# Loading the later fixed expert weights pair by pair instead of in groups of four pairs

## What is computed

```
x = x + attn_a(layernorm(x));  x = x + ffn(layernorm(x))
x = x + attn_b(layernorm(x));  x = x + ffn(layernorm(x))      # the same ffn weights

# ffn, with n = 2048 tokens, E = 64 experts, 256 -> 64 -> 256 features
g = silu(einsum('nd,edf->nef', flat, wg))
u = einsum('nd,edf->nef', flat, wu)
routed = einsum('ne,nef,efd->nd', comb, g * u, wd)
shared = einsum('nsh,shd->nd', silu(flat @ swg) * (flat @ swu), swd)
```

## Time and profile before

| | |
|---|---|
| time, median of 3 executions | 1133.81 us (1128.94, 1133.81 and 1746.06) |
| the profiled execution's own time | 1126.66 us |
| its span, first to last instruction | 1125.1 us |
| PE busy | 906.6 us (81%) |
| DVE busy | 706.6 us (63%) |
| POOL busy | 554.8 us (49%) |
| ACT busy | 465.3 us (41%) |
| 16 DMA engines, queue of SP (q1) | 42.7% busy, 111.40 MB |
| granted TensorE clock, mean | 0.90 |

### The profile page before, as it was taken

One profiled execution on the slowest core, in us unless ns is written; L12 is line 12 of the kernel. 1 busy time (PEld: TensorE's weight loads), 2 busy tenths in 40 slices (PEclk: granted clock), 3 DMA queues, 4 the chain that ended last, 5 costly groups with the idle time before them and its releaser, 6 DMA issues. The chain is left out here.

```text
span 1125.1 us, 24059 instructions
## 1 busy us (share of the span) xinstructions
PE 906.6 (81%) x7450; PEld 685.9 (61%) x7450; DVE 706.6 (63%) x2262; ACT 465.3 (41%) x978; POOL 554.8 (49%) x831
## 2 busy tenths in 40 slices
PE   6995999988876999976866999997977798995600
PEld 5772666667765777855654455476766576884500
DVE  6888888867922565435656999759852265544432
ACT  3662656541102555542635688831100354551000
POOL 3001244438886333337881444348877532325786
PEclk9996999998988999997987799997979899998765
DMA  7386999919995999732587887109233699763333
GB/s 264 58 163 118 206 236 239 259 45 307 249 242 178 292 304 284 238 110 84 141 196 156 126 115 119 19 3 293 102 104 112 197 293 309 240 203 107 111 108 103
DMA packets 159166, 197.88 MB, mean 176 GB/s; under 512 B 17377, under 2 KB 137697, under 8 KB 155873
## 3 DMA queue, kind: packets, MB, share of 16 engines
q1 hardware_dynamic: 118688, 111.40, 42.7%
q0 software_dynamic: 22848, 68.18, 18.9%
q10 hardware_dynamic: 17504, 16.78, 4.5%
HBM read 132.86 MB, written 90.18 MB: 198 GB/s over the span
## 5 line engine op out<-in xcount | busy, mean ns | idle before, releaser
L981 ACT ACTIVATE tmp<-ps 128x256 f32<-128x256 f32 (+1 forms) x344 | 155.8, 477 | 103.4 <-PE ps L922 47.9
L1111 ACT ACTIVATE tmp<-ps 128x384 f32<-128x384 f32 (+1 forms) x256 | 134.9, 543 | 61.6 <-PE ps L710 38.4
L537 POOL DMA_INDIRECT xd<-big,slot x128 | 128.0, 1000 | 46.9 <-POOL pause_at L451 36.0
L489 POOL COPY arena<-negmax 24x2048 bf16<-24x2048 bf16 x32 | 60.5, 1890 | 134.1 <-ACT negmax L981 92.0
L577 POOL DMA_INDIRECT spill<-yd,slot x96 | 99.0, 1032 | 33.2 <-POOL pause_at L451 22.8
L619 PE MATMUL ps<-arena 96*128 96x256 bf16 (+1 forms) x512 | 98.8, 280 | 16.1 <-DVE tmp L1332 6.9
L707 PE MATMUL ps<-arena 120*128 120x256 bf16 (+1 forms) x512 | 101.4, 265 | 0.5 <-ACT tmp L1111 0.2
L1335 DVE TENSOR_REDUCE tmp<-ps 128x2 f32<-128x512 f32 x128 | 81.8, 684 | 10.7 <-PE ps L619 10.6
L1263 DVE SCALAR_TENSOR_TENSOR X<-spill,comb,X 128x256 f32<-128x256 f32 x96 | 45.6, 486 | 67.6 <-DMA spill<-yd,slot 67.4
L1678 DVE SCALAR_TENSOR_TENSOR tmp<-tmp,ps 128x128 f32<-128x128 f32 x128 | 36.7, 287 | 79.8 <-ACT tmp L1189 79.1
L1688 DVE COPY tmp<-ps 128x256 f32<-128x256 f32 x128 | 52.3, 423 | 53.3 <-PE ps L951 29.8
(11 more groups left out here) (199 smaller groups left out, 1983.6 us busy)
## 6 DMA issues: line engine op xcount, KB each, us to landing
big<-xd POOLq DMA_DIRECT2D x128, 256.0 KB, 4.4
arena<-parts SPq DMA_DIRECT2D x192, 128.0 KB, 5.3
xd<-zero SPq DMA_DIRECT2D x8, 2048.0 KB, 14.4
spill<-in_we SPq DMA_DIRECT2D x128, 128.0 KB, 3.3
yd<-tmp POOLq DMA_DIRECT2D x64, 256.0 KB, 3.3
yd<-tmp ACTq DMA_DIRECT2D x64, 256.0 KB, 3.5
arena<-in_we SPq DMA_DIRECT2D x14, 1024.0 KB, 6.6
yd<-zero SPq DMA_DIRECT2D x8, 1024.0 KB, 22.5
```

The costliest lines, as they stand in the source:

```text
L537: pool.indirect_dma_start(xd[:, :], bass.IndirectOffsetOnAxis(ap=slot[:, i, k:k + 1], axis=0), xn_all[:, i, :], None).then_inc(scattered.s ...
L981: return act.activation(dst, src, ACT.Copy)
L1111: act.activation(prob[h % 8][:, 0:n], ps[2 + h % 2][:, 0:n], ACT.Exp).then_inc(exp_ready.sem, 1)
```

## The change

Before, after every fourth finished pair SP loads a whole group of four fixed pairs: one transfer of 1 MB for gate and up and four of 128 KB for down. This happens three times in a pass, at `done` = 3, 7 and 11. Now, after each of the first 12 finished pairs, SP loads the one fixed pair that takes the place that has just come free: one transfer of 256 KB for gate and up and two of 64 KB for down. Bytes are the same. The first 20 fixed pairs are still loaded by groups. PE still waits for all four pairs of a group at once, with new counts: 80 for a group loaded in one go (5 transfers of 16), and 48 for each pair (3 of 16).

```diff
-        fixed_in = [signal(f"fixed_in{i}", 80 * len(range(i, FGROUPS, FSLOTS))) for i in range(FSLOTS)]
+        fixed_in = [signal(f"fixed_in{i}", 80 + 48 * GROUP * (i + FSLOTS < FGROUPS)) for i in range(FSLOTS)]
...
+        def load_pair(e, m):
+
+            i = m % FRING // GROUP
+            e.dma_start(fixed_gu[m % FRING], t["we"][2 * m:2 * m + 2, :, 0:4 * FF].rearrange("e p n -> p e n")).then_inc(fixed_in[i].sem, 16)
+            for half in range(2):
+                e.dma_start(fixed_d[m % FRING][FF * half:FF * half + FF].rearrange("f (a n) -> f a n", a=2),
+                            t["we"][2 * m + half, :, 4 * FF:].rearrange("(a f) n -> f a n", a=2)).then_inc(fixed_in[i].sem, 16)
...
                     load_over(m)
                     done = m - RING
-                    if done % GROUP == GROUP - 1 and done + FRING < FIXED:
-                        load_fixed(sp, (done + 1 + FRING) // GROUP - 1)
+                    if done + FRING < FIXED:
+                        load_pair(sp, done + FRING)
...
-                        pe.wait_ge(*fixed_in[m // GROUP % FSLOTS](r, 80 * (m // FRING + 1)))
+                        pe.wait_ge(*fixed_in[m // GROUP % FSLOTS](r, 80 + 48 * GROUP * (m // FRING)))
```

## The result

| | before | changed |
|---|---|---|
| time, median | 1131.84 us | **1149.43 us** (1148.55 to 1152.16, 4 executions) |
| ratio | | **1.016**, 95% interval 1.012 to 1.020 |
| profiled execution, its span | 1126.66, 1125.1 us | 1149.91, 1148.4 us |

The change costs 18 us (the two profiled executions are 23.3 us apart). The interval ends at the 2% line, so it is slower without doubt, and most likely by less than 2%. One of the four executions of before took 1746 us; the ratio leaves it out.

What follows compares the result with a forecast made beforehand. SP's issuing was taken to bound the stage for twelve steps, making pair 16 9.4 us late: 4.3 us lost in pass 1 and 0.7 in pass 2, sum +5. Forecast 1136 us, range 1122 to 1152.

Steps and rivals of the forecast that it cites:

- Mechanism: Expert stage: SP's issuing becomes the bound for twelve steps and overflow weights come late; 0 to +15 us, chance 0.70.
- likeliest class: Whole kernel: time the same within 2%, some 23 us; chance 0.93.
- dearest sum: Pair loads at 2.17 us and landing at 5.6: pair 16 is 14.3 us late, sum +15 us.
- rival C: SP's queue: long table reads after pair loads, +9 us in one pass, sum +14, or +23 in both; chance 0.18.
- SP's time for twelve steps: SP's queue from t0, pair 0's `ed_done`: twelve overflow loads and twelve pair loads at 1.85 us each, 62.0 us.
- upper price: SP's queue: each down issue of a pair load at 0.86 us, making a pair load 2.17.
- pair 6 is nearly 2 us late: PE's wait for overflow weights: pair 6 nearly 2 us late, each second pair after it adding 2.4.
- Landing: Overflow weights of pair 16: last transfer lands some 4.5 us after its start, between calm and burst medians.
- rival B: Expert stage: issues cost nothing that matters, bursts gone, both delays vanish, -13.8 us; in part or whole, chance 0.12.
- SP's lag of 1 us per group: Kernel before: four steps with a group need 17.1 us of SP where PE gives 15.9, so SP falls behind.
- The fixed 2 us: Small down transfers: if about 2 us fixed cost fell on SP for each of 21 more, some 40 us a pass.

Runs made afterwards that it cites:

- group of two: The kernel before, with a group's down weights in one transfer from a row-by-row copy, 2 issues per group in place of 5: 1128.0 us, 0.995.
- rows on ACT: Changed kernel with all down weights from a row-by-row copy and pair loads issued from ACT's queue: 1116.3 us, 0.982 of before; repeat 1118.1 us, 0.985.
- pairs on ACT: Changed kernel with the same pair loads issued from ACT's queue in place of SP's: 1122.4 us, 0.991 of before.
- few bytes: Changed kernel with an eighth of the bytes in each pair load, same transfers and rows: pass 1 delay 16.1 us; no time compared.
- few rows: Changed kernel with each pair-load transfer cut to 16 partitions, an eighth of the rows: pass 1 delay 10.6 us; no time compared.
- no pair loads: Changed kernel with the call of `load_pair` taken out: pass 1 delay 0; span of its one execution 1113.3 us.

## Why the prediction was right, and where not

**Mechanism: right.** SP became the bound, the stalls moved to the overflow weights of pairs with data, the stall on results not yet stored went, the DMA share fell. The time, 1149.4, lies in the range of 1122 to 1152, near its top; within 2% was the likeliest class. That it lies inside is partly luck: 18 us is more than the +15 of the dearest sum, and the range reached it only by the part given to rival C, which did not come.

**The size of the sum: too small.** +5 was forecast, 18 measured, 22.5 by the delays of the two profiles. The term that was mis-sized is SP's time for twelve steps, 6 x (4.06 + 2.58) + 12 x 1.85 = 62.0. It took 70.8 and 67.2, and pair 16 came 18.1 and 15.1 us late where 9.4 was forecast. The steps with an empty pair were right: most took 4.43 to 4.5 us, and 2.58 + 1.85 is 4.43. The steps with data were forecast at 5.91 and took 7.1 us on average in pass 1 and 6.7 in pass 2, none below 6.06. Each has seven issues with work behind them, and in most steps one or two were long by 0.3 to 1.3 us, like the 1.49 shown above. The first issue of a pair load was also 0.59 us after a pair with data and 0.40 after an empty one. I had the long issues in view (a maximum of 4443 ns in rows 7, 0.86 as an upper price), and put them only in the upper end. They belonged in the middle: a queue that never rests passes all of them on. A queue with time to spare takes them in: without pair loads SP had an issue of 1.04 us at 408.08 and four table reads over 0.5 us in these steps, and no delay.

One step of the working doesn't follow from the sum: "pair 6 is nearly 2 us late". With 2.4 us from one second pair to the next and 9.4 at pair 16, pair 8 is just in time, pair 6 is 2.4 us early and pair 10 is the first late one. Measured in pass 1, pair 6 was 1.4 and pair 8 was 4.4 us late; in pass 2 pair 6 was in time and pair 8 was 2.5 late. Nor did each second pair add the same: pair 14 came without a stall in both passes.

**The long table read (rival C): a small part.** It was over 0.5 us after four pair loads in pass 1 and three in pass 2, about 2 us in pass 1 and 1 in pass 2, not 9. C's condition of 2.6 us per load, table read included, was not met: in pass 1 the loads average 2.1, or 2.3 with what the table reads took over 0.28.

**Landing: right.** Pair 16's last transfer started at 437.98 and PE went on at 442.17, 4.2 us later against the 4.5 taken.

**The clock: not forecast.** After the 4.15 us stall at pair 16 the next 16 matmuls took 1.98 us in place of 1.04, and the delay grew from 18.1 to 19.5; in pass 2 from 15.1 to 16.8. The granted clock behind the stall was 0.50, the level of 1.2 GHz (busy times by stretch):

```profile
442.20:444.00 1.80, 1.80 (x16) 1.54 (x16) 0.00 (x0) 0.00 (x0) 0.00 (x0) 0.50 0.28 82
```

The granted clock in 904 to 967 us was 0.92 where before's was 0.97. While SP was the bound this cost nothing, I take it, as SP did not wait for PE; behind the last stall it cost 1.4 and 1.7 us.

**Relief (rival B): there is something to win, but not by this change.** Without pair loads the delays are zero, so B's ceiling of 13.8 us was about right (12 by the spans). My account of before, SP's lag of 1 us per group and overflow weights that land late, was incomplete. With SP kept up the delays stayed, on the stores behind the burst. That did not change the sum, since the delay was taken as measured.

**The pages.** The Trainium skill (DMA: Bandwidth & Descriptors, Issuing engines are not separate DMA queues) calls the sequencer's time usually small relative to the DMA. For one transfer this trace agrees (0.6 us against 4.2). For a queue that issues seven such in a step with data it was the bound: some 16 of 19.5 us. The fixed 2 us that the prediction took from this page is given there for transfers issued from GpSimd; on SP no issue of the new form took more than 1.4 us, and most took 0.6.

**Left open:** what makes an issue long. It is not the bytes in flight: with an eighth of them (DMA share 0.66) steps with data still took 6.8 us. It is not the number of issues in the pair load: it stayed with two. The best lead is the 16 KB packets of the queue "q8 instruction". I counted SP's non-empty issues up to about pair 16 in the changed kernel and in seven of the others (all but the group of two and rows on ACT), in both passes or, for pairs on ACT, few bytes, few rows and no pair loads, in pass 1. Of 89 that overlap such a packet, 28 took over 0.5 us more than the median of their line; of 561 that overlap none, 10 did. So most long issues lie over a packet, also the 1.49 us one above (packet from 412.65), but not all: the second down issue of the load at 382.23 took 1.18 us with none beside it. No experiment moved these packets, so that they are the cause is not shown.

## What to carry to other kernels

Before splitting a transfer into smaller ones, add up the issue times of the queue that gets them, per step of the pipeline, and compare the sum with the step: here 0.67 us was to spare and 1.85 was added. If the queue has no room, put the new issues on another queue or give the data a layout that needs fewer and simpler transfers; then, as here, spreading the bytes can pay. And for a queue that will be busy without a break, reckon with mean issue times, not with the calm ones.

## What the runs showed of the hardware

- An issue costs by its form, not by its bytes: 0.62 us for 64 partitions of two 512 B rows, the same with rows of 64 B; 0.42 us for 16 partitions of two; 0.40 for 128 partitions of two 1 KB rows (0.59 right after a pair with data); 0.47 for 128 partitions of one 1 KB row from the second copy.
- Issues on SP's and ACT's queues can end together after 1.3 to 1.6 us in place of 0.35 to 0.49, in the cases looked at while a 16 KB packet of the queue "q8 instruction" was under way; without one ACT's took 0.65 in place of 0.49. The Trainium skill (DMA: Bandwidth & Descriptors, Queues, rings and completion order) says that the two have rings of their own but no descriptor generator of their own; that both end at one moment agrees, and the long times of both may as well come from the packet.
- PE's stalls of 4.01 and 4.15 us were followed by a stretch at a granted clock of 0.50, the level of 1.2 GHz: 1.98 us in place of 1.04 for 16 matmuls. After stalls of 2.36 to 2.83 us these took 1.22 to 1.36 and the transposes behind them 1.97 in place of 1.09; after one of 1.22 us the same matmuls took 1.09.
- SP's issues that overlapped a 16 KB packet of the queue "q8 instruction" were long in 28 of 89 cases, the others in 10 of 561; stores behind a burst of 1.5 MB took 8.6 and 10.1 us (pass 2), where the median of ACT's stores after the last burst of pass 1 is 3.3 us.
